# Spreading the setup of a four-layer transformer kernel over its first attention stage

## What is computed

```python
x = x + _L0_xattn_ref(_layernorm(x), ctx, ctx, mask0, wo_w, wo_b)     # scores = q k^T + mask, relu(ctx @ wo.T + b)
x = x + _L0_ffn_ref(_layernorm(x), ...)                               # 8 experts, the best two of each token
x = x + _L1_xattn_ref(_layernorm(x), ctx, ctx, mask1, wq, wk, wv, wo, ...)
x = x + _L1_ffn_ref(_layernorm(x), clip_x, clip_down, w_gate, w_up, w_down)   # see below
x = x + _L2_xattn_ref(...);  x = x + _L2_ffn_ref(...)                 # the second: routing to 64 slots and a GRU
x = x + _L3_xattn_ref(...);  x = x + _L3_ffn_ref(...)                 # the second: shared and routed experts

def _weight_fake_quant(w):                                            # of w_gate, w_up (352 x 128), w_down (128 x 352)
    scale = max(abs(w), axis=1) / 127
    return clip(round(w / scale), -128, 127) * scale
gate = xq @ fake_quant(w_gate).T;  up = xq @ fake_quant(w_up).T
out = act_fake_quant(silu(gate) * up, clip_down) @ fake_quant(w_down).T
```

## Time and profile before

| | us |
|---|---|
| median of 3 runs | 2100.3 |
| lowest and highest | 2093.86, 2102.59 |
| the profiled execution | 2098.33 |
| its span, first to last instruction | 2096.5 |

### The profile page before, as it was taken

The page is one execution under the profiler, slowest core; times in us unless marked ns, Lnnn a source line. Parts: engine busy times, 40 slices in busy tenths (PEclk is TensorE's granted clock), DMA queues, the critical chain, the costliest instruction groups (busy, mean ns, idle before and its releaser), DMA issues.

```text
span 2096.5 us, 50110 instructions
## 1 busy us (share of the span) xinstructions
PE 1850.7 (88%) x17731; PEld 1506.8 (72%) x17731; DVE 1484.3 (71%) x3865; ACT 1304.1 (62%) x4466; POOL 621.6 (30%) x618
## 2 busy tenths in 40 slices
PE   2998999989999987777789889999999998888879
PEld 2877888778878775656666667777778776777665
DVE  5898887878878886757766675767757565655456
ACT  1987766656757786556677756666666654544432
POOL 0003031222412220033434343353443423333321
PEclk9999999999999999978899999999999999999999
DMA  8013355454644100400000021223212223232351
GB/s 247 17 32 106 118 162 151 117 158 137 175 142 142 30 27 24 143 15 20 30 7 15 6 66 46 81 67 98 93 54 70 82 79 91 83 98 74 104 158 41
DMA packets 128790, 178.45 MB, mean 85 GB/s; under 512 B 10144, under 2 KB 89824, under 8 KB 128288
## 3 DMA queue, kind: packets, MB, share of 16 engines
q1 hardware_dynamic: 120864, 159.51, 25.2%
q0 software_dynamic: 7680, 15.74, 2.4%
HBM read 141.26 MB, written 33.95 MB: 84 GB/s over the span
## 4 chain that ended last, share of the span: by engine, by line
PE 38%; DVE 9%; ACT 5%; issue 4%; POOL 1%; DVEq 0%; ACTq 0%
PE ps L1672 5%; PE ps L1969 5%; PE ps L1917 3%; PE ps L1722 3%; PE ps L1910 3%; PE ps L1706 3%; ACT pb L2118 2%; PE ps L1891 2%; PE ps L1713 2%; PE ps L1683 2%; PE ps L1732 2%; DVE nm L2497 1%; PE ps L1740 1%; PE ps L1939 1%; PE ps L1883 1%
## 5 line engine op out<-in xcount | busy, mean ns | idle before, releaser
L2118 ACT ACTIVATE pb<-ps,nm 128x128 f32<-128x128 f32 x1024 | 364.1, 378 | 194.3 <-DVE nm L2497 194.3
L2166 POOL TENSOR_TENSOR pb<-pb,rcs 128x512 f32<-128x512 f32 x256 | 268.8, 1051 | 657.9 <-DVE rcs L2505 657.2
L986 ACT ACTIVATE pb<-pb,nm 128x128 f32<-128x128 f32 x1024 | 312.9, 393 | 32.2 <-DVE nm L1221 30.4
L2522 DVE COPY pt<-ps 128x512 f32<-128x512 f32 x128 | 88.3, 690 | 197.9 <-PE ps L1969 197.8
L2118 ACT ACTIVATION_READ_ACCUMULATOR pb<-ps,nm 128x1 f32 x1024 | 222.3, 217 | 0.0
L2497 DVE TENSOR_REDUCE nm<-ps 128x8 f32<-128x1024 f32 x128 | 155.9, 1218 | 60.7 <-PE ps L1917 38.6
L1969 PE MATMUL ps<-w,pb 128*128 128x128 f32 x1024 | 167.1, 288 | 23.2 <-ACT pt L2126 10.8
L1221 DVE TENSOR_REDUCE nm<-pb 128x8 f32<-128x1024 f32 x128 | 156.2, 1220 | 4.4
L1969 PEld LDWEIGHTS ps<-w,pb 128*128 128x128 f32 x1024 | 121.2, 147 | 47.1 <-ACT pt L2126 20.3
L870 PE MATMUL ps<-w,pb 128*128 128x128 f32 x1024 | 141.2, 279 | 7.7 <-ACT pb L986 7.3
L2126 ACT ACTIVATE pt<-ps 128x512 f32<-128x512 f32 x128 | 77.0, 602 | 92.9 <-PE ps L1969 92.7
(11 more groups left out here) (381 smaller groups left out, 4403.0 us busy)
## 6 DMA issues: line engine op xcount, KB each, us to landing
big<-in_we SPq DMA_DIRECT2D x92, 514.0 KB
big<-in_we SPq DMA_DIRECT2D x109, 384.0 KB
sorted_out<-big SPq DMA_DIRECT2D x27, 256.0 KB
big<-sorted_in SPq DMA_DIRECT2D x7, 960.0 KB, 6.3
sorted_in<-big SPq DMA_DIRECT2D x4, 1472.0 KB, 12.2
big<-sorted_in SPq DMA_DIRECT2D x20, 256.0 KB, 3.6
hidden<-h_all SPq DMA_DIRECT2D x7, 512.0 KB, 2.9
h_all<-hidden SPq DMA_DIRECT2D x7, 512.0 KB, 3.8
```

The costliest lines, as they stand in the source:

```text
L986: m = a.activation(pb[:, n % 2, k * S:(k + 1) * S], pb[:, n % 2, k * S:(k + 1) * S], ACT.Exp, bias=nm[:, n % 2, k:k + 1])
L2118: m = a.activation(pb[:, n % 2, e * S:(e + 1) * S], ps[:, score_bank(n) + half, k * S:(k + 1) * S], ACT.Exp, bias=nm[:, n % 2, e:e + 1], a ...
L2166: g_.tensor_tensor(p4, p4, r4.unsqueeze(2).to_broadcast([P, 4, S]), ALU.mult).then_inc(n2["p_normed"], 1)
L2522: v.tensor_copy(pt[:, p % 2, 4 * S:8 * S], ps[:, BANK_T, :]).then_inc(n2["p_lo"], 1)
```

## The change

- SP loads in block 1 only the four batches of group 0 and the first 136 columns of `w` (the identity and the two head masks, moved to its front). The second group, the rest of `x_all`, the rest of `w`, `rows`, the weight blocks and the rank constants are issued in block 2, behind the loads of stream 0; the zeros for `sorted_in` behind those of stream 1. Pool clears `xs0` in place of VectorE, ahead of the first layer norm's power.
- Block 1 keeps the small memsets and no longer waits for anything. In block 2 VectorE waits for the first loads and starts with the layer norm of group 0; TensorE makes two more transposes of the identity ahead of it.
- Weight block t is handled at unit n = 5, 7, 9, 11, 13, 15, 17: VectorE makes its scale at place 3 of n (`scale_weight`: three operations), Pool rounds it (`round_weight`: three operations), TensorE transposes it at place 2 of n+1 into bank 5, and VectorE copies it out at place 2 of n+2 (`keep_weight`). The scale row follows at units 19 and 20. At n = 5 the engines wait for the loads.
- The slot constants are made at n = 128, 129 and 130 in the drain (`slot_constants`), the sigmoids at n = 131.
- The statistics of group 1 move from unit 0 to unit 1, its power and `apply` from unit 1 to unit 2.

```diff
           ("wvs", 128), ("wos", 128), ("slot", 128), ("slot_scale", 1), ("rw3", E3),
-          ("hm", 4), ("hms", 4), ("below", E0 * E0)]
+          ("below", E0 * E0)]
+W_FIRST = 128 + 4 + 4
 
...
-                sp.dma_start(w[:, :], w_d).then_inc(small_loaded, 16)
...
-                sp.dma_start(x_all[:, :, :], x_d.rearrange("b s d -> s b d")).then_inc(large_loaded, 16)
-                sp.dma_start(big[:, CONST:CONST + RANK_CONST], rank_d).then_inc(large_loaded, 16)
-                sp.wait_ge(sorted_zero, 1)
-                for g in range(NP):
-                    sp.dma_start(xs_d[g].rearrange("(t p) d -> p t d", p=P), xs0[:, :, :]).then_inc(xs_zeroed, 16)
-                sp.wait_ge(large_loaded, 16 * n_large)
+                sp.dma_start(x_all[:, 0:G, :], x_d.rearrange("b s d -> s b d")[:, 0:G, :]).then_inc(first_loaded, 16)
+                sp.dma_start(w[:, 0:W_FIRST], w_d[:, 0:W_FIRST]).then_inc(first_loaded, 16)
...
                 v.memset(sel_z[:, :, :], 0.0)
-                v.memset(xs0[:, :, :], 0.0).then_inc(sorted_zero, 1)
                 v.memset(gsc[:, :], 0.0)
                 v.memset(usc[:, :], 0.0)
-                v.wait_ge(small_loaded, 16 * n_small)
-                v.tensor_copy(identb[:, :], ident).then_inc(w_rounded, 1)
...
+        WEIGHTS_AT = [5, 7, 9, 11, 13, 15, 17]
+        DIAG_AT = WEIGHTS_AT[-1] + 2
+        SLOTS_FROM = NUN
+
+        def weight_rows(t):
+            return P if t == 6 else CH1[t % 3][1]
+
+        def weight(t):
+            return hT[0:weight_rows(t), 2, 0:FF1] if t == 6 else hT[0:weight_rows(t), t // 3, t % 3 * D:(t % 3 + 1) * D]
+
+        def rounded_weight(t):
+            return hT[0:weight_rows(t), 3, P + 192 * (t % 2):P + 192 * (t % 2) + 192].bitcast(BF16)
+
+        weights_turned = ps[:, 5, 0:256].bitcast(BF16)
+        diag = hT[:, 3, 0:P]
...
                 loads(0)
+                sp.dma_start(x_all[:, G:2 * G, :], x_d.rearrange("b s d -> s b d")[:, G:2 * G, :]).then_inc(second_loaded, 16)
+                sp.dma_start(x_all[:, 2 * G:B, :], x_d.rearrange("b s d -> s b d")[:, 2 * G:B, :]).then_inc(large_loaded, 16)
+                sp.dma_start(w[:, W_FIRST:W_N], w_d[:, W_FIRST:W_N]).then_inc(small_loaded, 16)
+                sp.dma_start(rows[:, :], r_d.partition_broadcast(P)).then_inc(small_loaded, 16)
+                for k, src in enumerate((wg_d, wu_d)):
+                    for c, (at, m) in enumerate(CH1):
+                        sp.dma_start(weight(3 * k + c), src[at:at + m, :]).then_inc(small_loaded, 16)
+                sp.dma_start(weight(6), wd_d).then_inc(small_loaded, 16)
+                sp.dma_start(big[:, CONST:CONST + RANK_CONST], rank_d).then_inc(large_loaded, 16)
                 for n in range(NUN):
                     j, u = divmod(n, NU)
                     if u == 0 and j + 1 < NST:
                         loads(j + 1)
+                    if n == 0:
+                        sp.wait_ge(sorted_zero, 1)
+                        for g in range(NP):
+                            sp.dma_start(xs_d[g].rearrange("(t p) d -> p t d", p=P), xs0[:, :, :]).then_inc(xs_zeroed, 16)
...
+                    if n == WEIGHTS_AT[0] and place == 0:
+                        pe.wait_ge(small_loaded, 16 * n_small)
+                        pe.wait_ge(large_loaded, 16 * n_large)
+                    if n - 1 in WEIGHTS_AT and place == 2:
+                        t = WEIGHTS_AT.index(n - 1)
+                        m, src = weight_rows(t), rounded_weight(t)
+                        pe.wait_ge(w_rounded, 1 + t + 1)
+                        if t < 6:
+                            i = pe.transpose(weights_turned[:, 0:m], src[:, 0:D], identb[0:m, 0:m])
+                        else:
+                            for c, (at, mc) in enumerate(CH1):
+                                i = pe.transpose(weights_turned[0:mc, c * P:(c + 1) * P], src[:, at:at + mc], identb[:, :])
+                        i.then_inc(w_turned, 1)
+                    if n == DIAG_AT + 1 and place == 0:
+                        pe.wait_ge(w_scaled, 8)
+                        pe.matmul(ps[:, 5, 0:P], ones[:, :], diag, start=True, stop=True).then_inc(w_turned, 1)
+                    if n == SLOTS_FROM + 1 and place == 2:
+                        pe.wait_ge(slots_ready, 1)
+                        pe.transpose(ps[:, 0, 0:P], hs_c[:, :], ident)
+                        pe.matmul(ps[:, 0, P:P + 1], hs_c[0:SLOTS, :], ones[0:SLOTS, 0:1], start=True, stop=True)\
+                            .then_inc(slots_psum, 1)
+                    if n == SLOTS_FROM + 2 and place == 2:
+                        pe.wait_ge(slots_ready, 2)
+                        pe.matmul(ps[0:HR, 1, 0:1], W("w1m"), smean[:, :], start=True, stop=True)
+                        pe.matmul(ps[:, 1, P:P + 3 * D], hsT[:, :], W("whh"), start=True, stop=True).then_inc(slots_psum, 1)
+
+                pe.wait_ge(first_loaded, 32)
+                for i in range(2):
+                    pe.transpose(ps[:, 4, i * P:(i + 1) * P], ident, ident)
                 turn_y(front, 1, (front.yT_ready, 1))
...
+                    if n == WEIGHTS_AT[0] and place == 0:
+                        a.wait_ge(small_loaded, 16 * n_small)
+                    if n == NUN + 3 and place == 2:
+                        a.activation(sc[:, 6:7], R("clip_x"), ACT.Sigmoid)
+                        a.activation(sc[:, 7:8], R("clip_down"), ACT.Sigmoid)
...
+                def round_weight(t):
+                    m, src = weight_rows(t), weight(t)
+                    g_.wait_ge(w_scaled, t + 1)
+                    wlink(g_.tensor_scalar(src, src, sc[0:m, 2:3], MAGIC, ALU.mult, ALU.add))
+                    wlink(g_.tensor_scalar(src, src, MAGIC, None, ALU.subtract))
+                    g_.tensor_scalar(rounded_weight(t)[:, 0:FF1 if t == 6 else D], src, QMAX, -QMAX - 1.0,
+                                     ALU.min, ALU.max).then_inc(w_rounded, 1)
+
+                wlink = linker(g_, setup_g, 2)
+
                 def gather(g, ks):
...
+                g_.memset(xs0[:, :, :], 0.0).then_inc(sorted_zero, 1)
...
                     if layer == 1 and u == 0:
                         gather(g, range(G, 2 * G))
-                    if layer == 0 and u == 1:
+                    if n == WEIGHTS_AT[0]:
+                        g_.wait_ge(small_loaded, 16 * n_small)
+                    if layer == 0 and u == (1 if j else 2):
...
+                    if n in WEIGHTS_AT:
+                        round_weight(WEIGHTS_AT.index(n))
...
                     layer, g = stream(j + 1)
-                    if n == 0 and place == 3:
+                    if n == 1 and place == 3:
+                        v.wait_ge(second_loaded, 16)
                         stats(front, 1, 2)
                     if stream(j + 2)[0] == 0 and here == (3, 7):
                         stats(front, g + 1, g + 2)
-                    if layer == 0 and here == (3, 1):
+                    if layer == 0 and here == (3, 1 if j else 2):
                         v.wait_ge(front.yT_psum, g)
                         apply(front, g, g + 1)
...
+                    if place == 2 and n - 2 in WEIGHTS_AT:
+                        keep_weight(WEIGHTS_AT.index(n - 2))
+                    if place == 3 and n in WEIGHTS_AT:
+                        if n == WEIGHTS_AT[0]:
+                            v.wait_ge(small_loaded, 16 * n_small)
+                            v.wait_ge(large_loaded, 16 * n_large)
+                        scale_weight(WEIGHTS_AT.index(n))
+                    if place == 3 and n == DIAG_AT:
+                        v.tensor_scalar(diag, ident, sc[:, 0:1], None, ALU.mult).then_inc(w_scaled, 1)
+                    if place == 2 and n == DIAG_AT + 1:
+                        v.wait_ge(w_turned, 8)
+                        v.tensor_copy(dscB[:, :], ps[:, 5, 0:P])
+                    if place == 3 and n - SLOTS_FROM in range(3):
+                        slot_constants(n - SLOTS_FROM)
                     for item in tiles_at(place - 1, n) if place in (1, 2) else tiles_at(2, n - 1) if place == 0 else ():
                         tile(*item)
 
+                def scale_weight(t):
+                    m, src = weight_rows(t), weight(t)
+                    scale = usc[0:m, t - 3:t - 2] if 3 <= t < 6 else (gsc[0:m, t:t + 1] if t < 3 else sc[0:m, 0:1])
+                    wlink(v.tensor_reduce(sc[0:m, 1:2], src, AX, ALU.max, apply_absolute_value=True))
+                    wlink(v.tensor_scalar(scale, sc[0:m, 1:2], 1.0 / QMAX, None, ALU.mult))
+                    v.reciprocal(sc[0:m, 2:3], scale).then_inc(w_scaled, 1)
+
+                def keep_weight(t):
+                    m = weight_rows(t)
+                    v.wait_ge(w_turned, t + 1)
+                    if t < 6:
+                        at = CH1[t % 3][0]
+                        v.tensor_copy((wgq if t < 3 else wuq)[:, at:at + m], weights_turned[:, 0:m])
+                    else:
```

(15 more changed lines are left out.)

91 lines of the change are left out of this document (15 added, 76 removed).

## The result

The changed kernel takes 2080.3 us (median of 8 runs, 2075.1 to 2088.3) against 2098.9 us for the kernel before (median of 8, 2093.9 to 2104.5): a ratio of 0.9907, with a 95% interval of 0.9887 to 0.9927. By that ratio it is 19.5 us less, with 15 to 24 in the interval; the two medians are 18.6 apart. The forecast was 2079 and the range 2069 to 2088. A second set of runs of the same two kernels gave 2080.8 against 2098.8, ratio 0.9907 again (0.9882 to 0.9932). One execution of the kernel before took 3523 us, against 2092 to 2121 for all its others, and is left out everywhere.

A forecast was written before the change was run, and what follows sets the result against it. The prediction saw a serial chain bounding the first 35 us, then three nearly full engines in attention. Terms -30.1 + 4.7 + 4.3 = -21.1 us gave 2079 us, range 2073 to 2085, over all cases 2069 to 2088.

The forecast's parts named there:

- Term 1: Start: the chain ahead of the first layer norm goes, which starts at 4.6 instead of 34.71; gain 30.1 us.
- C: Start: SP's bulk shares the DMA engines, so the first load lands late, at 13.4; 2088 us, chance 0.06.
- D: Attention units: instruction fetches come late while DMA engines are full; slower than before, 2117 us with three; chance 0.03.
- Term 2: Units 5 to 21: the weights' work on VectorE costs 4.7 us, bounds 0 and 7.3.
- these five cost in full: Units 7, 9, 13, 15, 17: VectorE's time is filled, so added weight work costs 4.7 us.
- The sign that I named: Maxima of unit 5 some 30 us earlier than before, those of unit 21 only some 25.
- Term 3: Drain, units 128 to 130: the slot constants are on the path and cost 4.3 us, bounds 2.0 and 5.8.
- Rival B: All moved work counts, 7.3 and 5.8 us, plus a TensorE low-clock stretch of 5; 2088 us, chance 0.16.
- A: The spread work is hidden and the drain's waits cover the slot constants; 2070 us, chance 0.13.

The follow-up runs named there:

- r2_before: The kernel before, unaltered, profiled once more: 2093.8 us, one execution.
- e1: Changed kernel with the slot constants moved from the drain to units 6, 8, 19 (VectorE) and 7, 14 (TensorE): 2077.0 us, median of 4.
- r4_same: The changed kernel, unaltered, run once more in the same job as e7: 2080.8 us, median of 6.
- e6: Changed kernel with only the early start: weights' rounding and slot constants left out, results set to 1; 2068.0 us, ratio 0.9825 to the kernel before.
- e7: The kernel of e1, unaltered, run again in the same job as r4_same: 2075.6 us, median of 6.

## Why the prediction was right

**What bounds the kernel.** Right. The first stretch was a serial chain and could go whole; the second had no room to give work away free.

**Term 1, the start: 30.1 forecast, 30.8 measured.** The first statistics came at 3.91, not 4.6. The load of 256 KB beside 68 KB of `w` landed within 3.2 us of its issue, at the short end of the two rows that I used, and the choice in between was 0.7 too careful. Pool's clearing cost nothing, as forecast, with a little more to spare than forecast (2.55 us, not 3.0). The full DMA queues took nothing from the attention units that now run beside them (from unit 3 to 4 and from 4 to 5 they take 4.14 and 4.34 us, as in the kernel before): rivals C and D are out. SP's own queue was where the bulk showed, with issues that lasted 6.70 us at 5.25 and 18.16 at 18.93, and nobody waited for them. Unit 5 stood 32.7 earlier: 31.2 at unit 0, and 1.5 because in the profile of before TensorE's clock rose later (its first record of full clock is at 56.2 us, that of r2_before at 51.4). r2_before, 1.95 ahead there, shows that this is the execution's and not the change's.

**Term 2, the weights: 4.7 forecast, 2.2 measured.** This is the term that was mis-sized, inside its bounds of 0 and 7.3. The step that failed is "so these five cost in full". The five steps got longer by 0.70, 0.65, 0.56, 0.34 and 0.91 us, 3.2 in all. First, the price was too high: by the rows of the changed kernel a scale costs 0.58 us and a copy 0.14, not 0.70 and 0.2, which makes 3.8 us of VectorE in the five units. Second, the `apply` at unit 9 gets 0.3 us shorter because Pool's copy moves away from it, though VectorE then waits 0.24 for scores. Third, units 13 and 15 were not filled: without the weights VectorE waits about a quarter of a us in each. Last, delay is regained: 0.64 us at unit 9, whose mask had waited 0.63, and 0.33 at units 19 and 20. My check of the path, that ScalarE waits for unit 8's maxima, went one unit on, and the next unit had the idle time. The sign that I named (unit 21 only 25 us earlier) failed in size, with 28.5. Pool's contention, taken as nothing for the mask, was nothing.

**Term 3, the slot constants in the drain: 4.3 forecast, 4.5 measured** in the profile, 3.2 to 4.7 over four executions, 4.4 taken back by e1. The path was as written: ScalarE's output copies wait 1.5 us more in sum, TensorE's values behind them, and then VectorE for the slot product. The size is in part luck. The price came from the setup, where the product took 1.65 us, the length that it has at the 1.2 GHz level in the profile after (0.91 in r4_same at full clock). The 1.00 in the clock column of that window does not speak against it: the trace's first record of the clock is at 56.2 us, and what lies ahead of it prints as 1.00. In the drain the product took 1.65 again, since the clock fell there. The forecast had no such fall; the longer gap that the constants open comes with it. Where the clock held (r4_same), the term is 3.2.

**The sum: -21.1 forecast, -19.4 in the profile.** The terms that are the change's own give -31.2 (unit 0's maxima) + 2.2 + 0.4 for the scale row + 4.5 = -24.1. The rest, 4.7 us, is the difference of the two executions elsewhere: -1.5 in the first units, +1.6 at unit 20, +2.1 between units 21 and 127, +2.4 in the feed-forward, +0.1 behind it. The first two are the clock's, as shown above; that the others are is likely and was not shown piece by piece.

The forecast named low-clock stretches as what could make it wrong, "in either direction", and put nothing for them in the sum. Over many executions they have one direction. The changed kernel spends 24 us more at 1.2 GHz (156 against 132), which at 0.37 us for each makes 9 us, an estimate from the table above. Its own terms with the clock up, term 3 at 3.2, are -25.4; with the 9 they make about -16, against a measured difference of the means of 17.4 us (14.1 to 20.7). From e6 to the changed kernel the own terms are 5.8 us and the clock's 21 us make 8, so 14, and the means are 15.9 apart.

So the total was right by luck in part. With the clock up, term 2 was 2.5 too large, term 3 1.1 too large and the start 1.1 too small, and the clock's cost, which the sum left out, made up for these and more. About half of the 24 us goes with the place of the slot constants, by e1 and e7, and the stretch in the drain is part of it; where the rest comes from stays open. Rival B priced such a stretch at its own length; at unit 20 it cost 1.6 us, and over whole executions 0.35 to 0.39 of its length.

**The rivals.** A (all hidden) is out by units 5 to 20 and by the drain. B (all counts, and one clock fall more) is out in its first half: 2.2 and 4.5 us, not 7.3 and 5.8. Its second half has something in it. Not at unit 20, where the fall comes with the moved work and without it (e6, r2_before), but in the drain and in the count over all executions.

## What to carry to other kernels

In this kernel the work on the serial chain at the start was worth its whole length, and the best place for it was a unit in which the engine waits anyway; count such waits in the following units too, since a delay is regained at the next idle gap. Read the ends of a pipeline as full stretches: in the drain little covers an added step, and the same constants (5.8 us in the setup) cost 3.2 to 4.7 us there and 0.5 to 1.3 among the early units. Price moved work by the clock of the place that it goes to, not of the place that it comes from, and look at what its waits do to TensorE: here, by the estimate above, the clock's share of the loss was at least as large as that of the moved work itself. The mean granted clock of many executions shows this where single profiles do not.

## What the runs showed of the hardware

- TensorE's low-clock stretches are not fixed to the code. Of four profiles of the changed kernel two were granted 0.66 between 280 and 300 us, one 0.91 and one 0.99, and filler that removed one stretch was followed by another 40 us later. The spans of these four profiles reach from 2077.2 to 2092.6; by their mean clocks (0.965 to 0.956) they spent 147 to 184 us at the lower level, and 37 us at 0.37 each would make 14 of these 15 us, an estimate. The Trainium skill ("TensorE: Matmul & The Clock Gate", Part 1) says that the number of slow matmuls at a start varies between runs of one kernel; the traces agree, and show the same far behind the start.
- How much of them a kernel has does depend on its code: 132 us on average before, 156 after. In the drain the clock fell in six of seven profiles in which TensorE had waited 2.15 us and in none of six in which it had waited 1.32.
- A first load of 256 KB in pieces of 512 bytes, with one of 68 KB behind it, was there 3.2 us after its issue at 0.73.
- An SP issue lasts 0.4 us on quiet queues and up to 6.70 us a DMA when the queues are full (`w` at 5.25); four DMAs together took 18.16.
- Of the two VectorE operations that were seen both beside Pool and alone, only the one within SBUF slowed: the mask with a PSUM operand kept its 1.22 us beside Pool's rounding, and `apply`, SBUF to SBUF, went from 1.11 to 1.40 beside Pool's copy.
